# GAT merge of a four-layer graph kernel: two accumulators of three planes, one for VectorE and one for Pool, joined by TensorE in the division

## The chip, the cores and the metric

The kernel runs on one core of one Trainium2 chip. The time is the device time of that core in microseconds, the median of three runs. A profile is one further execution, taken by the hardware profiler, and has its own time.

Engine names: PE is TensorE (PEld are its weight loads), DVE is VectorE, ACT is ScalarE, POOL is GpSimd (Pool), SP issues the transfers.

## The reference, cut to what matters

3125 nodes with 128 features and 103125 edges (`src`, `dst`, sorted by `dst`, self loops included) pass four layers: a graph convolution, an additive attention, a GAT with two heads, and a SchNet-like interaction. The change is in the GAT (and in buffers that the layers share):

```python
xl = (h @ Wl + bl).reshape(n, H, D)          # H = 2, D = 128
xr = (h @ Wr + br).reshape(n, H, D)
e = jax.nn.leaky_relu(xl[src] + xr[dst], NEG_SLOPE)
alpha = jnp.einsum('ehd,hd->eh', e, att)
alpha = _segment_softmax(alpha, dst, n)      # exp(a - max) / (sum + 1e-16) over each dst
msg = xl[src] * alpha[..., None]
out = jax.ops.segment_sum(msg, dst, num_segments=n).mean(axis=1)
out = out + h @ res_W + bias
return residual + out
```

## The kernel before, in words

Nodes are padded to N = 3200 (25 blocks of 128). Edges are cut into 202 tiles of 512. As `dst` is sorted, a tile touches a window of WIN = 20 neighbouring nodes, whose first node is the tile's base (`base_i`). Where all edges lie in their windows one pass does (`k.passes` is 1 at run time); otherwise the stages of a layer run once for each window offset, in a device loop.

**Stages.** A `Stage` is a block with its own semaphores; all engines meet at its end. The GAT layer is: two normalisations, `project` ("sides", which also clears accumulators), `attend` (the attention loop), `merge_gat`, `divide_gat`.

**The attention loop** (`attend`, L1940) goes over the 202 tiles in a software pipeline (`over_tiles`), where each engine works in one step at different tiles. Pool gathers source rows (L888) into a ring of eight buffers; TensorE makes scores, weights and sums; VectorE finds the greatest score of a tile and head. For each tile it leaves three things: `partial`, the weighted sums of the tile's window for each head (128 features on the partitions, 20 columns a head), with weights exp(score - tile's top); `weight_sum`, the sums of the weights; and the tile's tops. Two VectorE instructions keep the tops (`best_of_nodes`): L2220 copies the tile's top in each window cell from PSUM to `rows`, and L2223 takes the running maximum of each node into `node_top`.

**The merge** (`merge_gat`, L2251) brings all tiles to the nodes' common top. Tiles go in groups of GROUP = 24 (`over_groups`): eight full groups and one of ten. The body gets several groups at once, each some rounds behind; the first and last rounds are unrolled, the middle ones are a device loop over pairs of rounds. Columns of a group are its tiles' windows side by side, 24 x 20 = 480. For one group:

- *lower* (L2272): for each tile, 2x20 elements, its row of tops minus `node_top` at its window. VectorE does the first 12 tiles, Pool the other 12.
- ScalarE takes the exponential of the group's row (L2335).
- *columns* (`scale_columns`, L2242): VectorE spreads `weight_sum` over the cells, 128x480.
- *spread*: TensorE spreads each head's factors to 128 partitions with a row of ones (L2348, two matmuls, each profiled as two records) and turns the columns into rows of sums (L2350).
- VectorE multiplies the sums' row by the factors (L2306, 2x480) and `partial` by them, one head at a time (L2310, 128x480, in place).
- *add*: for each tile, VectorE adds 128 x 2 x 20 to `acc` at the window (L2322), and Pool adds 2x20 of the sums' row to `node_sum` (L2363). An engine's adds go one after the other, each waiting for the one before, as neighbouring windows can overlap.

A round lowers the group `now` and adds the group `past`, two groups behind. VectorE and Pool each do 24 adds and 12 lowerings a round, in three batches of eight adds and four lowerings; ahead of a batch the engine reads its 12 window bases from memory into registers (`window_bases`). In a round `now`'s columns are made after these two waits:

```python
dve.wait_ge(spread_ready, past.g + 1)      # TensorE has spread group `past`
wait_count(dve, spread_ready, now.g - 1)   # the columns' buffer (two halves) is free
```

**The division** (`divide_gat`, L2411). TensorE turns the row sums (25 blocks of 2x128, L2425), and then, in seven chunks of up to four blocks, three planes of each: both heads of `acc` and the residual part in `fb` (L2433, 75 transposes). VectorE takes the inverses, adds the residual plane (L2472) and the first head times its inverse (L2476); ScalarE multiplies the second head (L2444), and Pool adds it to `x` (L2455). Chunks alternate between two sets of banks.

Another stage has a role in the prediction: `collect_sums` (L2936), which adds three tables with fp32 matmuls against the identity, `start` on the first and `stop` on the last (L2964, four blocks and three tables a unit). In `project`, VectorE's L635 and Pool's L673 subtract rounded pieces, both with two operands in SBUF.

## Time and profile before

| | |
|---|---|
| median of three runs | 4929.67 us (4923.24 to 4929.72) |
| the profiled execution | 4951.51 us, its span 4949.7 us |
| attention loop of the GAT | 2058.0 to 3406.8 us of the span |
| merge | 3406.8 to 3534.4 us |
| division | 3534.4 to 3553.5 us |
| busy over the span | PE 3993 us (81%), DVE 2863 (58%), ACT 1738 (35%), POOL 2830 (57%) |
| granted TensorE clock | 0.85 mean; 1.0 is 2.4 GHz, 0.5 is 1.2 GHz |

A row of the timeline gives the start, the busy time, the engine, the line and operation, output and inputs, the count, and in brackets the idle time before it and what ended that. A row of a source line gives the least, median and greatest duration in ns. Starts are in us from the start of the span. A row of a stretch gives its bounds and length, then for PE, PEld, DVE, ACT and POOL the busy time and (x) the instructions, and last the granted clock, the DMA share and GB/s. A row of costliest groups gives busy time in us and mean ns, then the idle time ahead and what ended it.

### The profile page before, as it was taken

The page shows a single profiled execution, that of the slowest core. Times are in us where ns is not written, and L with a number is a line of the kernel's source. Part 1 is how long each engine was busy: PE and PEld are TensorE (multiplying, and loading weights), DVE is VectorE, ACT ScalarE, POOL GpSimd, SP SyncE. Part 2 cuts the span into 40 slices and gives each one's busy share as a digit, 9 for nine tenths or more (in the row PEclk, how much of TensorE's full clock was granted, in tenths as well). Part 3 has the DMA queues.
Part 4 walks back from the last instruction along what each step waited for, and adds up shares of the span by engine and source line. Part 5 has one row for each costly group of instructions (what it writes and reads, how often), then busy time and mean ns, then how long its engine had stood idle before and what let it go on. Part 6 is the DMA issues. An engine that isn't in the chain of part 4 may idle for free. (4 is left out here: it accounts for less than half of the span.)

```text
span 4949.7 us, 89651 instructions
## 1 busy us (share of the span) xinstructions
PE 3993.3 (81%) x22463; PEld 2250.2 (45%) x22566; DVE 2862.7 (58%) x8478; ACT 1738.1 (35%) x4474; POOL 2829.9 (57%) x3055
## 2 busy tenths in 40 slices
PE   3996927878878787488888888886479999999987
PEld 1344424444444454244444444442246556556652
DVE  7994032333333334555555555555678888888868
ACT  3773033344344344333333333331222222222226
POOL 0122355666666663555555555554368888888862
PEclk8997967777777777688888888887689999999999
DMA  2322522222222221333333333331056666666660
GB/s 79 97 80 87 160 70 55 57 55 57 55 56 56 56 57 29 110 87 95 96 94 95 95 96 93 95 95 31 1 106 104 105 104 104 104 105 104 105 109 14
DMA packets 377425, 402.41 MB, mean 81 GB/s; under 512 B 86457, under 2 KB 322502, under 8 KB 377030
## 3 DMA queue, kind: packets, MB, share of 16 engines
q0 software_dynamic: 151904, 198.72, 20.8%
q1 hardware_dynamic: 225382, 202.21, 14.3%
q8 instruction: 43, 0.70, 0.1%
q14 instruction: 96, 0.79, 0.1%
HBM read 312.91 MB, written 87.78 MB: 81 GB/s over the span
## 5 line engine op out<-in xcount | busy, mean ns | idle before, releaser
L888 POOL DMA_INDIRECT gathered<-table,sources x952 | 907.0, 953 | 611.8 <-issue 258.9
L1676 POOL DMA_INDIRECT sums<-gathered,idx x606 | 989.9, 1634 | 217.1 <-issue 166.7
L1538 PE MATMUL bank<-wide 128*128 128x512 bf16 x3533 | 829.1, 379 | 5.6 <-issue 0.2
L2195 DVE TENSOR_REDUCE neg_raw<-bank 80x1 f32<-80x512 f32 (+1 forms) x404 | 276.7, 685 | 727.5 <-DMA dst_pair<-local_rows 277.4
L888 POOL DMA_INDIRECT wide<-table,sources x464 | 440.0, 948 | 284.4 <-issue 123.6
L2145 ACT ACTIVATE msg<-bank,neg_top 80x512 f32<-80x512 f32 (+1 forms) x404 | 275.9, 683 | 716.6 <-issue 376.0
L1538 PEld LDWEIGHTS bank<-wide 128*128 128x128 bf16 x3636 | 347.7, 98 | 364.1 <-issue 1.6
L1212 POOL TENSOR_TENSOR acc<-acc,msg 128x20 f32 x404 | 108.7, 269 | 419.6 <-issue 245.7
L2188 DVE TENSOR_TENSOR zact<-zact,bank 128x512 f32<-128x512 f32 x404 | 259.5, 684 | 121.8 <-ACT zact L2137 79.8
L2073 PE MATMUL bank<-zact,att_cells 128*32 128x512 f32 x808 | 287.5, 750 | 46.6 <-issue 45.8
L2055 PEld LDWEIGHTS bank<-ident,gathered 128*128 128x128 f32 x1360 | 196.6, 169 | 272.3 <-issue 248.9
L2076 PE MATMUL bank<-zact,att_cells 128*80 128x512 f32 x404 | 302.7, 841 | 9.2 <-issue 9.2
L2213 DVE COPY edge_rows<-bank 128x320 f32<-128x320 f32 (+1 forms) x404 | 183.3, 454 | 179.1 <-remote 109.2
L2055 PE MATMUL bank<-ident,gathered 128*128 128x128 f32 x1360 | 243.7, 322 | 35.6 <-issue 23.8
L2111 PE MATMUL bank<-edge_rows,gathered 128*128 128x80 f32 x1088 | 185.1, 326 | 102.2 <-DVE edge_rows L2213 91.6
L888 POOL DMA_INDIRECT h_nm<-table,sources x200 | 190.4, 952 | 133.5 <-DMA wide<-table,sources 68.1
L1159 DVE TENSOR_SCALAR gathered<-iota_c,partial 128x500 f16<-128x500 f16 x812 | 265.1, 349 | 2.4 <-issue 1.4
L2086 PE MATMUL bank<-ident,msg 80*128 80x80 f32 (+1 forms) x1616 | 209.3, 256 | 64.8 <-issue 29.0
L2157 ACT COPY partial<-bank 32x20 f32 (+1 forms) x808 | 133.1, 165 | 347.0 <-remote 250.5
L1168 PE MATMUL bank<-gathered,zact 128*128 128x500 f16 x812 | 209.2, 380 | 53.9 <-ACT zact L1275 28.2
L2137 ACT ACTIVATE zact<-bank 128x512 f32<-128x512 f32 x404 | 216.9, 588 | 94.7 <-DMA window<-parts 77.6
L1589 ACT COPY gathered<-bank 128x437 f32<-128x437 f32 x202 | 106.2, 525 | 336.7 <-PE bank L1564 245.3
(394 smaller groups left out, 7612.2 us busy)
## 6 DMA issues: line engine op xcount, KB each, us to landing
zact<-in_src_flat SPq DMA_DIRECT2D x202, 192.0 KB
edge_rows<-in_attr_rows SPq DMA_DIRECT2D x202, 128.0 KB
dst_pair<-local_rows SPq DMA_DIRECT2D x177, 128.0 KB
gathered<-table,sources POOLq DMA_INDIRECT x952
dst_pair<-local_rows SPq DMA_DIRECT2D x202, 64.0 KB
counts<-wide SPq DMA_DIRECT2D x4, 3000.0 KB
counts<-fm_ab SPq DMA_DIRECT2D x4, 3000.0 KB
fm_ab<-counts SPq DMA_DIRECT2D x4, 3000.0 KB
```

The source lines that it names most:

```text
L888: pool.indirect_dma_start(out=g[:, j, :], out_offset=None, in_=table, in_offset=bass.IndirectOffsetOnAxis(ap=mine, axis=0)).then_inc(rows_ ...
L1159: hot = dve.tensor_scalar(k.cell_hot[slot][:, j, :], k.iota_c[:, :], k.cell[:, q], None, ALU.is_equal)
L1538: pe.matmul(k.bank[b][:, :], k.split[t.two][:, c, :], k.source_hot[t.two][:, b * CHUNK:(b + 1) * CHUNK], start=first, stop=c == PARTS - 1, ...
L1676: pool.indirect_dma_start(out=k.sums[j], out_offset=bass.IndirectOffsetOnAxis(ap=k.idx[t.slot][:, j:j + 1], axis=0), in_=out_rows(t)[:, j, ...
L2055: pe.matmul(z_bank(t, h)[:, j * P:(j + 1) * P], g[:, j, h * F:(h + 1) * F], k.ident[:, :], is_transpose=True, start=(j == 0), stop=False, ...
L2073: mm = pe.matmul(score_bank(t)[own_cells(h), :], a.att[h][:, own_cells(h)], k.zact[t.two][:, h, :], start=False, stop=True, skip_group_che ...
L2076: mm = pe.matmul(score_bank(t), a.att[0][:, :], k.zact[t.two][:, 0, :], start=False, stop=True)
L2086: mm = pe.transpose(weight_bank(t)[:, j * cells:(j + 1) * cells], raised(t)[:, j * P:(j + 1) * P], k.ident[lanes(t), lanes(t)])
L2137: act.mul(k.zact[t.two][:, h, :], z_bank(t, h)[:, :], 0.2).then_inc(slope_ready, 1)
L2145: act.activation(raised(t), score_bank(t), ACT.Exp, bias=k.neg_top[lanes(t), bass.ds(t.t, 1)], accum_out=k.weight_sum[lanes(t), bass.ds(t. ...
L2188: m = dve.tensor_tensor(za, za, z_bank(t, h)[:, :], ALU.max)
L2195: dve.tensor_reduce(raw, score_bank(t), AX.X, ALU.max, negate=True).then_inc(top_found, 1)
```

## The change

- There are two accumulators of three planes (head 0, head 1, row sums on partitions 32 and 33): `planes`, the first three planes of one tensor `four` that now holds `acc`, `fa` and `fb`, and `more_planes`, in a new tensor `arena` that also holds `h`, the gathered rows, `dst_pair` and `onehot_t` of the attention loop. VectorE adds the first half of a group's tiles to `planes`, Pool the second half to `more_planes`, each in one instruction of 128 x 3 x 20.
- The scaled parts of a group are written to `scaled` (two halves) and no longer in place.
- The attention loop doesn't copy the tops to `rows`. The merge remakes them from `neg_top`: a second `scale_columns`, one more TensorE matmul and a ScalarE copy into `tops`. A round now has `ahead` (columns, tops), `now` one group behind (lowering, exponential, spread) and `past` three groups behind (multiply, add).
- Lowering adds `node_top` to the negative top, and the exponential has scale -1.
- Bases are read 12 at a time, twice a round.
- After the groups VectorE joins the first accumulator with the arena in a loop of `k.passes` steps of 60 columns and subtracts the arena's part from itself; with one pass this is one step.
- The division reads both accumulators: each transpose of a head or of the row sums becomes two accumulating matmuls against the identity.
- Clears move: Pool clears the arena in five pieces at the end of the attention loop, `node_top` is set at that loop's start on VectorE; `neg_top` is cleared in "sides", and the upper part of `dst_pair` in "xj".

```diff
-    k.h = k.sb("h_nm", [P, B, F])
-    k.fab = k.sb("fm_ab", [P, 2, N])
+    k.arena = k.sb("arena", [P, 3 * N])
+    k.h = k.arena[:, 0:N].rearrange("p (b f) -> p b f", f=F)
+    k.four = k.sb("four", [P, 4, N])
+    k.acc, k.fab = k.four[:, 0:2, :], k.four[:, 2:4, :]
     k.fa, k.fb = k.fab[:, 0, :], k.fab[:, 1, :]
-    k.acc = k.sb("acc", [P, 2, N])
+    k.planes, k.more_planes = k.four[:, 0:3, :], k.arena[:, :].rearrange("p (z n) -> p z n", z=3)
...
+                if gat:
+                    assert k.tiles % ring == 2 and ring == DEEP + 2
+                    n, at = k.n_nodes, k.ring_at
+                    pool.wait_ge(sums_ready, k.tiles - 6)
+                    pool.memset(k.arena[:, at[2]:at[4]], 0.0).then_inc(cleared, 1)
+                    pool.wait_ge(sums_ready, k.tiles - 2)
+                    pool.memset(k.arena[:, 0:n], 0.0).then_inc(cleared, 1)
+                    pool.wait_ge(score_ready, k.tiles)
+                    pool.memset(k.arena[:, at[4]:3 * n], 0.0).then_inc(cleared, 1)
+                    pool.wait_ge(sums_ready, k.tiles - 1)
+                    pool.memset(k.arena[:, at[0]:at[1]], 0.0).then_inc(cleared, 1)
+                    pool.wait_ge(sums_ready, k.tiles)
+                    pool.memset(k.arena[:, at[1]:at[2]], 0.0).then_inc(cleared, 1)
+                    pool.wait_ge(cleared, 5)
...
-                    dve.tensor_copy(k.rows[0:heads, bass.ds(t.t * WIN, WIN)], top_bank(t)).then_inc(top_kept, 1)
-                    wait_count(dve, best, t.t)
+                    dve.wait_ge(best, t.t + 1)
...
+        def lower_and_add(eng, now, past, side, planes):
+
+            for lo in range(0, share, batch):
+                lowers = range(0, 0) if now is None else range(lo, min(lo + batch, now.size // 2))
+                adds = range(0, 0) if past is None else range(lo, min(lo + batch, past.size // 2))
+                tops = window_bases(k, eng, now.t + side * now.size // 2 + lo, len(lowers)) if lowers else []
+                ends = window_bases(k, eng, past.t + side * past.size // 2 + lo, len(adds)) if adds else []
+                for n in range(batch):
+                    if n < len(adds):
+                        i = side * past.size // 2 + adds[n]
+                        wait_count(eng, added[side], past.g * share + adds[n])
+                        w = planes[:, :, bass.ds(ends[n], WIN)]
+                        eng.tensor_tensor(w, w, k.scaled[past.par][:, :, i * WIN:(i + 1) * WIN],
+                                          ALU.add).then_inc(added[side], 1)
+                    if n < len(lowers):
+                        i = side * now.size // 2 + lowers[n]
+                        if lowers[n] == 0:
+                            eng.wait_ge(tops_kept, now.g + 1)
+                            wait_count(eng, scaled, now.g - 1)
+                        m = eng.tensor_tensor(k.lowered[now.par][:, i * WIN:(i + 1) * WIN],
+                                              k.tops[now.par][:, i * WIN:(i + 1) * WIN],
+                                              k.node_top[:, bass.ds(tops[n], WIN)], ALU.add)
+                        if lowers[n] == now.size // 2 - 1:
+                            m.then_inc(lowered[side], 1)
...
+                def spread_and_add(ahead, now, past):
                     if past is not None:
                         n = past.size * WIN
+                        out = k.scaled[past.par]
                         dve.wait_ge(spread_ready, past.g + 1)
+                        wait_count(dve, added[0], (past.g - 1) * share)
+                        wait_count(dve, added[1], (past.g - 1) * share)
+                        dve.tensor_tensor(out[k.sum_lanes, 2, 0:n], k.lowered[past.par][:, 0:n],
+                                          k.bank[4 + past.par][0:heads, 0:n], ALU.mult)
                         for h in range(heads):
+                            m = dve.tensor_tensor(out[:, h, 0:n],
+                                                  a.partial[:, h, bass.ds(past.t, past.size), :].rearrange(
+                                                      "p t n -> p (t n)"),
+                                                  k.bank[h * 2 + past.par][:, 0:n], ALU.mult)
                         m.then_inc(scaled, 1)
+                    if ahead is not None:
+                        wait_count(dve, tops_ready, ahead.g - 1)
+                        wait_count(dve, spread_ready, ahead.g - 1)
+                        scale_columns(k, dve, a, top_columns(ahead), k.neg_top, ahead)
+                        scale_columns(k, dve, a, sum_columns(ahead), k.weight_sum, ahead).then_inc(columns_ready, 1)
                     if past is not None:
                         dve.wait_ge(scaled, past.g + 1)
+                    lower_and_add(dve, now, past, 0, k.planes)
+                over_groups(dve, k.tiles, (0, 1, 3), spread_and_add)
+                dve.wait_ge(added[0], total)
+                dve.wait_ge(added[1], total)
+                size = 3 * k.n_nodes // ceil_div(k.n_nodes, WIN)
+                mine = k.planes.rearrange("p z n -> p (z n)")
+                with dve.Fori(0, k.passes) as n:
+                    cols = bass.ds(n * size, size)
+                    dve.tensor_tensor(mine[:, cols], mine[:, cols], k.arena[:, cols], ALU.add).then_inc(joined, 1)
+                    dve.wait_ge(joined, n + 1)
+                    dve.tensor_tensor(k.arena[:, cols], k.arena[:, cols], k.arena[:, cols], ALU.subtract)
 
             @block.scalar
             def _(act):
+                def keep_and_raise(ahead, now):
+                    if ahead is not None:
+                        n = ahead.size * WIN
+                        act.wait_ge(tops_ready, ahead.g + 1)
+                        for eng_lowered in lowered:
+                            wait_count(act, eng_lowered, ahead.g - 1)
+                        act.copy(k.tops[ahead.par][:, 0:n], k.bank[6 + ahead.par][0:heads, 0:n]).then_inc(tops_kept, 1)
+                    if now is not None:
+                        m = k.lowered[now.par][:, 0:now.size * WIN]
+                        act.wait_ge(lowered[0], now.g + 1)
+                        act.wait_ge(lowered[1], now.g + 1)
+                        act.activation(m, m, ACT.Exp, scale=-1.0).then_inc(raised, 1)
+                over_groups(act, k.tiles, (0, 1), keep_and_raise)
 
             @block.tensor
             def _(pe):
+                def spreads(ahead, now):
+                    if ahead is not None:
+                        n = ahead.size * WIN
+                        pe.wait_ge(columns_ready, ahead.g + 1)
+                        wait_count(pe, tops_kept, ahead.g - 1)
+                        pe.matmul(k.bank[6 + ahead.par][0:heads, 0:n], a.own[:, :],
+                                  top_columns(ahead)[0:a.lanes, 0:n], start=True, stop=True).then_inc(tops_ready, 1)
+                    if now is not None:
+                        n = now.size * WIN
+                        pe.wait_ge(raised, now.g + 1)
+                        wait_count(pe, scaled, now.g - 1)
+                        for h in range(heads):
+                            pe.matmul(k.bank[h * 2 + now.par][:, 0:n], k.head_row[:, h * P:(h + 1) * P],
+                                      k.lowered[now.par][:, 0:n], start=True, stop=True)
+                        pe.matmul(k.bank[4 + now.par][0:heads, 0:n], a.own[:, :], sum_columns(now)[0:a.lanes, 0:n],
+                                  start=True, stop=True).then_inc(spread_ready, 1)
+                over_groups(pe, k.tiles, (0, 1), spreads)
...
                 for b in range(B):
-                    mm = pe.transpose(k.bank[7][:, b * heads:(b + 1) * heads], k.node_sum[:, b * P:(b + 1) * P],
-                                      k.ident[k.sum_lanes, k.sum_lanes])
+                    out, cols = k.bank[7][:, b * heads:(b + 1) * heads], slice(b * P, (b + 1) * P)
+                    pe.matmul(out, k.node_sum[:, cols], k.ident[k.sum_lanes, k.sum_lanes], start=True, stop=False)
+                    mm = pe.matmul(out, k.more_planes[k.sum_lanes, 2, cols], k.ident[k.sum_lanes, k.sum_lanes],
+                                   start=False, stop=True)
                 mm.then_inc(sums_turned, 1)
                 for i, (lo, hi) in enumerate(cs):
                     wait_count(pe, divided, i - 1)
                     wait_count(pe, headed, i - 1)
-                    for n, src in enumerate(srcs):
+                    for n in range(heads):
                         for b in range(lo // P, hi // P):
-                            mm = pe.transpose(k.bank[n * 2 + i % 2][:, b * P - lo:(b + 1) * P - lo],
-                                              src[:, b * P:(b + 1) * P], k.ident[:, :])
+                            out, cols = k.bank[n * 2 + i % 2][:, b * P - lo:(b + 1) * P - lo], slice(b * P, (b + 1) * P)
+                            pe.matmul(out, k.acc[:, n, cols], k.ident[:, :], start=True, stop=False)
+                            pe.matmul(out, k.more_planes[:, n, cols], k.ident[:, :], start=False, stop=True)
+                    for b in range(lo // P, hi // P):
+                        mm = pe.transpose(k.bank[heads * 2 + i % 2][:, b * P - lo:(b + 1) * P - lo],
+                                          k.fb[:, b * P:(b + 1) * P], k.ident[:, :])
                     mm.then_inc(ready, 1)
```

In the middle part the removed lines of the four engines' programs are left out; they are in the code above.

## Rows read from the trace of the kernel before

**Rows 1.** Busy time of each engine in three stretches: attention loop, merge, division.

```profile
2058.00:3406.80 1348.80, 1107.76 (x7683) 578.07 (x7683) 736.41 (x2025) 416.08 (x1018) 768.32 (x808) 0.86 0.33 93
...
3406.80:3534.40 127.60, 44.37 (x54) 11.21 (x54) 76.18 (x344) 5.18 (x9) 66.79 (x298) 0.50 0.00 1
...
3534.40:3553.50 19.10, 13.50 (x100) 12.21 (x100) 11.88 (x35) 7.13 (x25) 8.05 (x7) 0.83 0.00 1
```

**Rows 2.** Timeline of the merge, one group of tiles.

```profile
3458.34 0.64 DVE L2306 TENSOR_TENSOR zact<-wide,bank 2x480 f32<-2x480 f32 x1
...
3459.01 1.22 DVE L2310 TENSOR_TENSOR partial<-partial,bank 128x480 f32 x2
...
3459.52 0.60 ACT L2335 ACTIVATE wide<-wide  x1 [13.51 <-POOL wide L2272]
...
3460.15 0.65 DVE L2242 TENSOR_TENSOR msg<-weight_sum,place 128x480 f32<-128x480 f32 x1
...
3460.36 0.49 PEld L2348 LDWEIGHTS bank<-wide,head_row 2*128 2x128 f32 x2 [10.62 <-issue]
...
3460.36 3.56 PE L2348 MATMUL bank<-wide,head_row 2*128 x4 [8.95 <-DVE partial L2310]
...
3461.32 0.33 PEld L2348 LDWEIGHTS bank<-wide,head_row 2*128 2x128 f32 x1 [0.47 <-issue]
...
3463.85 1.76 PE L2350 MATMUL bank<-msg,own 128*2 128x480 f32 x2
```

**Rows 3.** Timeline of the merge, VectorE's adds, unrolled and in the loop.

```profile
3437.19 0.20 DVE L2322 TENSOR_TENSOR acc<-acc,partial 128x40 f32 x1 [0.94 <-DVE acc L2322]
...
3437.52 0.53 DVE L2322 TENSOR_TENSOR acc<-acc,partial 128x40 f32 x2
...
3466.61 0.20 DVE L2322 TENSOR_TENSOR acc<-acc,partial  x1 [0.17 <-DVE acc L2322]
...
3467.02 0.20 DVE L2322 TENSOR_TENSOR acc<-acc,partial  x1
```

**Rows 4.** Timeline of the merge, Pool's adds (a lowering between).

```profile
3470.05 0.21 POOL L2363 TENSOR_TENSOR fm_ab<-fm_ab,zact 2x20 f32 x1 [0.85 <-POOL fm_ab L2363]
...
3470.61 0.22 POOL L2363 TENSOR_TENSOR fm_ab<-fm_ab,zact 2x20 f32 x1
```

**Rows 5.** One source line: Pool's adds in the division.

```profile
L2455 POOL TENSOR_TENSOR x_nm<-x_nm,wide x7: 454/1272/1279, 3542.8 to 3552.8; 128x512 f32<-128x512 f32 x6, 128x128 f32<-128x128 f32 x1
```

**Rows 6.** Timeline of the division, TensorE.

```profile
3535.10 2.82 PE L2425 MATMUL bank<-ident,fm_ab 2*128 2x2 f32 x25 [17.54 <-PEq L909]
...
3544.54 1.06 PE L2433 MATMUL bank<-ident,acc 128*128 128x128 f32 x8 [0.26 <-DVE x_nm L2476]
```

**Rows 7.** Timeline of the stage that collects the sums, TensorE.

```profile
4818.45 1.95 PE L2964 MATMUL bank<-ident,wide 128*128 128x128 f32 x16
...
4821.13 1.95 PE L2964 MATMUL bank<-ident,wide 128*128 128x128 f32 x16
```

**Rows 8.** Busy time in two stretches: TensorE's clock in division and collection.

```profile
3538.00:3542.00 4.00, 4.00 (x24) 3.84 (x24) 2.00 (x6) 1.15 (x4) 0.00 (x0) 0.66 0.01 4
...
4814.00:4818.00 4.00, 3.82 (x20) 3.82 (x21) 0.00 (x0) 0.00 (x0) 0.00 (x0) 0.58 0.94 313
```

**Rows 9.** Timeline of the projection "sides", Pool and VectorE.

```profile
2045.97 1.16 POOL L673 TENSOR_TENSOR gathered<-gathered,h_nm 128x512 f32<-128x512 f32 x1 [1.01 <-ACT h_nm L653]
...
2046.45 1.23 DVE L635 TENSOR_TENSOR gathered<-gathered,h_nm 128x512 f32<-128x512 f32 x1 [0.28 <-ACT h_nm L656]
```

**Rows 10.** Costliest groups of the attention loop, two of VectorE's.

```profile
L2195 DVE TENSOR_REDUCE neg_raw<-bank 64x1 f32<-64x512 f32 x202 | 138.8, 687 | 313.1 <-DMA dst_pair<-local_rows 277.4 <-PE bank L2073 34.0
...
L2220 DVE COPY wide<-bank 2x20 f32 (+1 forms) x202 | 35.0, 173 | 15.7 <-DMA wide<-table,sources 1.7 <-issue 1.3 <-PE bank L2095 0.4
```

**Rows 11.** A source line of Pool's memsets, and the timeline of the loop's end.

```profile
L669 POOL MEMSET acc<- x2: 5433/5435/5437, 657.2 to 2016.3; 128x6400 f32 x2
...
3400.53 1.07 PE L2107 MATMUL bank<-h_nm,edge_rows 128*32 128x128 f32 x16
```

140 lines of the change are left out of this document (44 added, 96 removed).

## The prediction

> **What bounds the kernel now.** I began with the busy time by stretch [rows 1]. The profiled execution took 4951.51 us, 1.8 us more than its span. Three stretches touch the change. The GAT attention loop (1349 us) is untouched but for one VectorE instruction a tile and its last microseconds. The merge (127.6 us) is the stage that is rewritten. The division (19.1 us) gets more matmuls. In the merge TensorE runs at its lower clock (0.50) and is busy 44 us, VectorE 76, Pool 67: no engine is full, so what counts is who waits for whom.
>
> The timeline of one group of 24 tiles shows that [rows 2]. ScalarE idles 13.5 us and works 0.60, so a group takes 14.1 us. TensorE starts when the exponential is there and runs 3.56 + 1.76 us, 5.25 from first start to last end. Its result is wanted only in the next round, so this 5.25 lies beside VectorE's and Pool's own work. VectorE multiplies (0.64 + 1.22), makes one set of columns (0.65), then has 24 adds and 12 lowerings, as Pool has. An add, a lowering and an add start 0.33 us after each other where the code is unrolled and 0.41 in the loop [rows 3]; each new set of bases costs a gap of 0.94. Pool needs 0.56 for the same pair and a gap of 0.85 [rows 4]. Both engines are near their own limit.
>
> **The change part by part.**
>
> *Merge, the adds.* VectorE and Pool now have 12 adds and 12 lowerings each, in two batches. A VectorE add grows from 40 to 60 columns: 0.02 us more by the multiply of 480 in about 0.61 [rows 2], so a pair is 0.35 unrolled and 0.43 looped; 12 pairs and two gaps of 0.9 are 6.0 and 7.0 us. A Pool add goes from 2x20 (0.22) to 128x60. Pool's 128x512 and 128x128 adds take 1.27 and 0.45 [rows 5], 2.1 ns a column, so 60 columns are about 0.31 and a pair 0.67: with its start (1.3) and one gap a round is 10.2 us.
>
> *Merge, a new wait.* The row-sum columns are now made in the round of `ahead`, while the same group is lowered one round later (`now`). The buffer has two halves, so making columns for group g waits until TensorE has spread g-2, and g-2 was lowered at the end of the round just before. The old code made and lowered in one round and had a whole round of slack there. Behind this wait stand VectorE's columns, all its adds and its lowerings, and for these lowerings the next exponential waits. The loop is therefore serial: signal 0.2, exponential 0.60, signal 0.2, TensorE 5.25 [rows 2], 6.3 in all; the three multiplies (1.9) and Pool's share hide in it. Then two sets of columns, 1.3, then 6.0 or 7.0 of adds. A round is 13.6 unrolled and 14.6 in the loop, against 10.2 for Pool, which so has slack.
>
> The stage: columns, tops through TensorE and ScalarE and the first lowerings, about 7.1; chain 6.3, columns 1.3 and the next lowerings 2.9: 17.6 before the first adds. Six held rounds, three at 13.6, two at 14.6, one with a short last group at 13.0: 83.0. The last three rounds have no columns, and Pool, whose adds follow each other at 0.50 when nothing lies between, is last: 11 + 8 + 3.5 = 22.5. Joining the accumulators, one pass of a loop, is 2.5 by estimate from two 60-column operations (0.25 each) and its reads. Sum 125.6, against 127.1 from the stage's first to its last instruction.
>
> *Contention.* Pool's adds now have full width beside two-operand adds of VectorE. A VectorE operation of 128x512 with two SBUF operands took 1.23 us with a Pool operation beside it for 0.68 of that [rows 9]; by the multiply above it would be about 0.67 alone. So nearly the whole overlap was lost. Pool moves data some 0.13 us per add; a quarter to a half of these meet an add. I take 0.5 us a round, +3 (bounds 0 and +10, where Pool too becomes slower and the round is Pool's). The Trainium skill (GPSIMD Engine Reference, Specifications) says that Pool shares its SBUF interfaces with VectorE and contends with instructions that have two SBUF inputs; the trace agrees in this one row pair. The merge comes to +1.5.
>
> *Division.* 75 transposes and 25 small ones become 25 transposes and 150 matmuls, since a sum of two planes needs accumulating fp32 matmuls. The same form stands in the stage that collects the sums: twelve of them (four blocks, three tables) every 2.68 us at the full clock, 0.223 each [rows 7]; each is two records (16 for eight), where a transpose is one. Transposes are 0.133 each [rows 6]. A chunk of four blocks goes from 12 transposes (1.6, hidden under VectorE's 1.8) to 16 x 0.223 + 4 x 0.133 = 4.1. TensorE becomes the bound: 6 x 4.1 + 1.0 = 25.6. The row sums: 25 in 2.82 become 50 matmuls. At the low clock two weight loads of full form from two partitions span 0.49 and one takes 0.33 [rows 2], so they stand 0.17 apart and a matmul takes 0.34; at the full clock I take 0.22. The clock rose about 5.5 us after the stage's start [rows 6, 8]. 16 cold and 34 warm are 13.0. With 1.4 behind the last matmul: 40.0, against 18.2: +21.8. Lower bound: two loads at the transposes' pace (0.113), halved once warm, 8.3 for the row sums, +17. Upper: the clock rises only when wide matmuls come; in the other stage it stood at 0.58 over the first 4 us [rows 8]; 17.0 and 1.5 for a cold first chunk, +27.
>
> By the Trainium skill (TensorE: Matmul & The Clock Gate, LDWEIGHTS) a weight load goes by its columns, not its rows, 0.107 us for 128. The 25 small transposes agree (0.113 each). By that rule the row sums at two loads each would cost 10.7 and the division be 2.3 us shorter.
>
> *Attention loop.* The copy of the tops to `rows` goes (202 x 0.17) [rows 10]. VectorE idles there 313 us ahead of its first reduction, waiting for others; TensorE is busy 1108 of 1349 us. I take -2; bounds 0 and -38. The added memset of `node_top` (2x3200, about 2.7) lies in VectorE's wait for the first loads; its old place on Pool lay beside an equal one on VectorE: 0.
>
> *Clears on Pool at the loop's end.* Five memsets at 0.85 ns a column [rows 11]. The 3200 columns wait for the sums that end at 3401.6, then 2304, 1024 and 1024: 2.7 + 2.0 + 0.9 + 0.9 and signals is 3408.5, against 3406.6 now: +2 (bounds 0, +3). `neg_top` and `dst_pair` clears ahead of projections: +0.3, since Pool's first subtraction comes later anyway.
>
> Sum: -2 + 2 + 0.3 + 1.5 + 21.8 = +23.6. The profiled execution would be 4975. It lay 22 us above the median of the runs, so I move the median: 4929.7 + 23.6 = 4953.
>
> **The rivals.**
> - *The merge isn't held.* If the columns find TensorE done, a round is Pool's 10.2 to 10.8, six rounds save 19 to 20 us: +3, 4933, no change. For it: this is the overlap the two engines' counts would allow. Against: the wait's count and TensorE's 5.25.
> - *The division is cheap.* If the matmuls cost as transposes do, TensorE needs 5.5 for the row sums and 2.5 a chunk, +3 in place of +21.8: 4935, no change. Rows 7 speak against it.
> - *The copy sat on the attention loop's path.* Then each tile gains the copy and its start, 0.19: -38, in all -13, 4917, faster. It decides from 0.16 us a tile on. For it: the copy stands ahead of the weights that TensorE's sums need. Against: VectorE's 313 us of idle [rows 10].
> - *Pool and VectorE slow each other* beyond what I took: rounds of 15.2 set by Pool, +10: 4963, slower. By the skill's rule this is what two-input adds on both engines would do; the row pair shows the size only for wide operations.
>
> **How the numbers follow.** A measurement of this kernel can tell 0.2%, 10 us, from no change. Chances: forecast 0.66, contention 0.12, merge not held 0.07, division cheap 0.07, copy on the path 0.08. So slower 0.78, same 0.14, faster 0.08. The range goes from the two cases of no change, 4932, to 4968, the upper bound of the division with part of the contention; only the faster case and the sums of several extremes are left out. For the forecast alone it is 4944 to 4964.
>
> **What would show it.** In the profile after: `columns` (the second set) on VectorE idles about 4 us until the last matmul of the round, in six rounds; ScalarE's exponentials stay 13 to 15 us apart; Pool idles some 3 us a round on `scaled`; VectorE's adds take 0.22, Pool's 0.31. The division's stretch is near 40 us with TensorE full and VectorE waiting for it. The attention loop's length is unchanged within 3 us. Wrong it would be if the division's matmuls overlap better than in the stage I took them from, if the loop's length moves (202 tiles make 10 us of 0.05), or if Pool's full-width adds are far from 0.31.

## The result and the profile after

The changed kernel took 4968.09 us (median of 4, 4967.64 to 4969.75) against 4927.51 for the kernel before (now a median of 4 as well): the difference of the medians is 40.6 us. The ratio on record is 1.0088, 95% interval 1.0075 to 1.0100, that is 37 to 49 us slower. The direction was right, the size was not: +23.6 had been forecast, and the median lies 0.1 us above the range's upper end of 4968.

The profiled execution of after took 4969.75 us, 1.7 off its median; that of before had lain 22 us above its own. So the two profiles are compared stage by stage, not by their spans. Busy time by stretch of the kernel after (columns as in [rows 1]); attention loop, a stretch in between that was not there before, merge, division:

```profile
2045.80:3379.10 1333.30, 1107.33 (x7683) 578.58 (x7683) 710.85 (x1822) 414.21 (x1018) 772.58 (x812) 0.87 0.33 94
3379.10:3387.20 8.10, 0.00 (x0) 0.00 (x0) 0.00 (x0) 0.00 (x0) 1.62 (x2) 0.66 0.00 1
3387.20:3520.70 133.50, 59.08 (x72) 12.01 (x72) 62.37 (x249) 9.89 (x18) 52.92 (x202) 0.51 0.00 1
3520.70:3573.00 52.30, 48.32 (x325) 48.07 (x325) 13.06 (x39) 7.93 (x26) 8.02 (x7) 0.76 0.00 1
```

Read against [rows 1]. On one basis (first operation of a stage to the first of the next): VectorE's idle in front of the merge 0.32 before, 8.20 after; merge 128.2 (3406.91 to 3535.10) and 133.5; division 18.6 (3535.10 to 3553.73) and 51.5 (3520.76 to 3572.24). That is +7.9, +5.3 and +32.8, +46.0 in all, inside the interval of the medians. The attention loop is judged further down; from its first to its last copy of the sums it took 1286.9 us in the profile of before and 1271.6 in this one.

**In front of the merge.** Timeline of the loop's end: Pool's memsets and VectorE's operations on either side of the gap.

```profile
3374.20 2.77 POOL L2060 MEMSET arena<- 128x3200 f32 x1 [14.97 <-PE bank L2133]
...
3376.91 2.02 POOL L2062 MEMSET arena<- 128x2304 f32 x1
...
3378.87 0.96 POOL L2064 MEMSET arena<- 128x1024 f32 x1
3378.89 0.20 DVE L2254 COPY partial<-bank 128x40 f32<-128x40 f32 x1 [1.49 <-PE bank L2145]
3379.76 0.96 POOL L2066 MEMSET arena<- 128x1024 f32 x1
3387.29 0.66 DVE L2269 TENSOR_TENSOR edge_rows<-neg_top,place 128x480 f32<-128x480 f32 x1 [8.20 <-PEq L2035]
```

The bracket is VectorE's idle time ahead of the merge. The memsets take what was forecast and end 1.6 us behind VectorE. The other 6.6 us stand in a view that shows the engines' sequencers as well: the source line that opens the stage's block. Its columns are count, shortest, median and longest in ns, first and last start.

```profile
L2035 DVEq DRAIN  x1: 236/236/236, 3378.9 to 3378.9; - x1
L2035 POOLq COMPARE_BRANCH  x1: 33/33/33, 3380.8 to 3380.8; - x1
L2035 POOLq DRAIN  x1: 5881/5881/5881, 3381.1 to 3381.1; - x1
L2035 SPq EVENT_SEMAPHORE  x1: 17/17/17, 3387.2 to 3387.2; - x1
```

The same line of the kernel before:

```profile
L2022 POOLq DRAIN  x1: 9565/9565/9565, 3378.2 to 3378.2; - x1
L2022 ACTq DRAIN  x1: 289/289/289, 3405.7 to 3405.7; - x1
```

A drain is what an engine's sequencer records at the end of a stage. Here Pool's took 5.9 us after the change and 9.6 before, where the other engines' took 0.24 to 0.29. In both profiles only three of Pool's drains took more than 0.2 us, each at the end of a stage in which Pool gathers or scatters rows by index; what it waits for in them is not shown. Before, the drain ended 19 us ahead of the others' last. Now the clears stand in front of it, and everybody waits.

**The merge.** Timeline of the first held round after: VectorE's held columns, Pool beside them, the first adds.

```profile
3410.51 0.66 DVE L2269 TENSOR_TENSOR edge_rows<-neg_top,place 128x480 f32<-128x480 f32 x1 [4.15 <-PE bank L2391]
3410.53 0.79 POOL L2309 TENSOR_TENSOR arena<-arena,wide 128x60 f32 x1
3411.09 0.75 DVE L2269 TENSOR_TENSOR msg<-weight_sum,place 128x480 f32<-128x480 f32 x1
...
3412.39 0.22 DVE L2309 TENSOR_TENSOR four<-four,wide 128x60 f32 x1 [0.55 <-issue]
3412.60 0.17 DVE L2316 TENSOR_TENSOR wide<-wide 2x20 f32<-2x20 f32 x1
3412.75 0.22 DVE L2309 TENSOR_TENSOR four<-four,wide 128x60 f32 x1
```

The first add of each of the two batches in the last held round, then the exponentials in front of and behind the six held rounds:

```profile
3488.64 0.22 DVE L2309 TENSOR_TENSOR four<-four,zact 128x60 f32 x1 [1.10 <-issue]
...
3493.74 0.22 DVE L2309 TENSOR_TENSOR four<-four,zact 128x60 f32 x1 [2.68 <-issue]
```

```profile
3404.49 0.60 ACT L2372 ACTIVATE zact<-zact 2x480 f32<-2x480 f32 x1 [0.47 <-DVE zact L2316]
...
3495.88 0.60 ACT L2372 ACTIVATE zact<-zact 2x480 f32<-2x480 f32 x1 [7.10 <-DVE zact L2316]
```

The forecast wait is there: columns held 4.0 to 4.2 us in six rounds (and 6.3 in the first), a VectorE add takes 0.22 and Pool's 0.31, where [rows 3, 4] have 0.20 and 0.22. What is new is the 2.68 us between a round's two batches of adds, where the kernel before had 0.94 to 1.2. The exponentials at 3404.49 and 3495.88 have six rounds between them: 91.4, where 83.0 was forecast. Each round took 15.0 to 15.4 us, in the loop and outside it. Pool is slowed where VectorE makes columns: its add beside them took 0.79 us, not 0.31 (3410.53); Pool has slack there.

**The division.** TensorE's timeline: row sums (each of the fifty matmuls is two records), then wide matmuls cold and warm.

```profile
3530.17 0.56 PE L2460 MATMUL bank<-ident,four 2*128 2x2 f32 x2
3530.59 0.56 PE L2461 MATMUL bank<-ident,arena 2*128 2x2 f32 x2
3531.02 0.56 PE L2460 MATMUL bank<-ident,four 2*128 2x2 f32 x2
...
3542.18 0.80 PE L2470 MATMUL bank<-ident,four 128*128 128x128 f32 x2
...
3546.54 0.39 PE L2470 MATMUL bank<-ident,four 128*128 128x128 f32 x2
...
3546.76 0.39 PE L2471 MATMUL bank<-ident,arena 128*128 128x128 f32 x2
```

Row-sum matmuls start 0.427 apart (3530.17, 3530.59, 3531.02), so fifty take 21.3 us. Wide ones start 0.427 apart too at the lower clock, and 0.22 apart at the full one, as in [rows 7]; a chunk then takes 4.01. The clock by stretch (the number ahead of the last two of a line):

```profile
3536.00:3540.00 4.00, 4.00 (x21) 4.00 (x20) 0.00 (x0) 0.00 (x0) 0.00 (x0) 0.50 0.00 0
3542.00:3545.00 3.00, 3.00 (x15) 2.98 (x15) 0.87 (x3) 0.00 (x0) 0.00 (x0) 0.50 0.00 0
3545.00:3548.00 3.00, 3.00 (x27) 3.00 (x27) 0.00 (x0) 0.00 (x0) 0.00 (x0) 0.91 0.02 5
```

TensorE was busy without a gap for 21 us of row sums at 1.2 GHz, and went to 2.4 about 3 us after the wide matmuls began.

### The profile page after: what moved, and what is told of

Same layout as the page of the kernel before. It is cut to its first block and busy times, and to the rows that moved or that the text cites. A ratio compares the mean times of both kernels' runs of the same rounds, so it can differ in the third digit from the quotient of the medians.

```text
span 4968.0 us, 89212 instructions
## 1 busy us (share of the span) xinstructions
PE 4039.8 (81%) x22809; PEld 2286.2 (46%) x22809; DVE 2824.7 (57%) x8182; ACT 1743.0 (35%) x4483; POOL 2820.9 (57%) x2967
## 5 line engine op out<-in xcount | busy, mean ns | idle before, releaser
L901 POOL DMA_INDIRECT arena<-table,sources x1152 | 1094.6, 950 | 734.4 <-issue 310.5
L1689 POOL DMA_INDIRECT sums<-arena,idx x606 | 989.0, 1632 | 217.3 <-issue 168.9
L2082 PEld LDWEIGHTS bank<-ident,arena 128*128 128x128 f32 x1760 | 242.1, 164 | 314.3 <-issue 292.7
L1225 POOL TENSOR_TENSOR four<-four,msg 128x20 f32 x404 | 108.7, 269 | 420.8 <-issue 246.2
L2082 PE MATMUL bank<-ident,arena 128*128 128x128 f32 x1760 | 300.8, 315 | 33.9 <-issue 16.9
L1172 DVE TENSOR_SCALAR arena<-iota_c,partial 128x500 f16<-128x500 f16 x812 | 258.1, 337 | 2.7 <-issue 1.7
L2137 PE MATMUL bank<-edge_rows,arena 128*128 128x80 f32 x1088 | 182.3, 322 | 89.0 <-DVE edge_rows L2241 70.2
L1181 PE MATMUL bank<-arena,zact 128*128 128x500 f16 x812 | 209.6, 381 | 53.9 <-ACT zact L1288 28.1
L1457 DVE TENSOR_SCALAR arena<-arena,iota_w,always 128x512 bf16<-128x512 bf16 x556 | 233.0, 419 | 17.2 <-DMA arena<-local_rows 13.7
L1602 ACT COPY arena<-bank 128x437 f32<-128x437 f32 x202 | 106.1, 525 | 336.7 <-PE bank L1577 249.6
```

Of the source, the lines that this page charges most:

```text
L901: pool.indirect_dma_start(out=g[:, j, :], out_offset=None, in_=table, in_offset=bass.IndirectOffsetOnAxis(ap=mine, axis=0)).then_inc(rows_ ...
L1172: hot = dve.tensor_scalar(k.cell_hot[slot][:, j, :], k.iota_c[:, :], k.cell[:, q], None, ALU.is_equal)
L1457: return dve.tensor_scalar(hot, row, k.iota_w[:, 0:1], k.always[:, 0:1], ALU.is_equal, ALU.max)
L1689: pool.indirect_dma_start(out=k.sums[j], out_offset=bass.IndirectOffsetOnAxis(ap=k.idx[t.slot][:, j:j + 1], axis=0), in_=out_rows(t)[:, j, ...
L2082: pe.matmul(z_bank(t, h)[:, j * P:(j + 1) * P], g[:, j, h * F:(h + 1) * F], k.ident[:, :], is_transpose=True, start=(j == 0), stop=False, ...
```

## The experiments

They ran in three sets. In the first two the kernel before took 4400 to 4401 us, at a mean granted clock of 0.91, in the third 4956, at 0.85, so a run is compared with the kernel before of its own set alone. The attention loop, from its first to its last copy of the sums, took 992 to 995 us in the first two, at a granted clock of 0.99 to 1.00, and 1284 to 1286 in the third, at 0.87 to 0.88; merge and division don't differ so. The first and the third set carry the same chip number, so the chip alone does not explain the two levels, and their cause stays open. "Over before" is the difference of the medians; "idle" is VectorE's idle in front of the merge; "merge and division" runs from the merge's first operation to the start of the last batch statistic behind the division (151.5 in the first profile of before, 189.6 in that of after).

| run | over before, us | ratio, 95% interval | idle | merge and division |
|---|---|---|---|---|
| before_again | profile only | | 0.3 | 151.8 |
| after_again | +41.8 | 1.0096 (1.0079 to 1.0113) | 8.2 | 189.6 |
| e1_unheld | +25.3 | 1.0058 (1.0041 to 1.0075) | 8.2 | 168.0 |
| e2_sums_by_dve | +33.2 | 1.0081 (1.0065 to 1.0098) | 8.2 | 175.1 |
| e3_two_clears | +41.2 | 1.0098 (1.0081 to 1.0115) | 4.1 | 190.0 |
| e4_batches_of_4 | +27.2 | 1.0063 (1.0047 to 1.0080) | 8.2 | 172.7 |
| e5_sums_third | +47.3 | 1.0110 (1.0093 to 1.0126) | 8.2 | 191.4 |
| e6_after_with_copy | +44.8 | 1.0104 (1.0087 to 1.0121) | 8.2 | 189.6 |
| e7_clears_in_merge | +33.1 | 1.0066 (1.0046 to 1.0085) | 0.3 | 190.8 |
| e8_loads_of_8 | +49.2 | 1.0094 (1.0073 to 1.0116) | 8.2 | 193.2 |
| e9_pool_joins_a_head | +18.2 | 1.0044 (1.0029 to 1.0059) | 8.1 | 167.6 |
| e10_all | -24.8 | 0.9952 (0.9936 to 0.9968) | 0.3 | 126.3 |

**The two kernels again.** No edit.

> The kernel before, unchanged, for a second profile. The first profiled execution of it took 4951.5 us against a median of 4929.7. If those 22 us lie in the attention loop, this one shows a loop some 20 to 26 us shorter than 1349 (1323 to 1329) and the same merge (128) and division (19) within 0.3 us; then the change's cost can be read stage by stage. If they lie in the merge or the division, those two stages are shorter here, and the change cost more in them than the two profiles show.

> The changed kernel, unchanged, beside the kernel before on the chip of this set, as the base for the other runs of the set. From the stages read so far: 8.2 us of gap in front of the merge against 0.3, the merge 133.5 against 128.2, the division up to the last batch statistic 56.1 against 23.3, the attention loop unchanged; so 44 to 48 us slower than the kernel before.

Merge and division of before came out as in its first profile (128.1 and 18.9). The loop, between its first and its last copy of the sums, took 993.0 us here, and 991.9 in the changed kernel. The second profile stands at the shorter level and so does not say where the 22 us of the first lay; the difference of 18.2 us between the two first spans is the stages' +46.0 less some 28 us ahead of the merge, which the medians do not confirm.

**The copy in the attention loop.**

```diff
                     dve.wait_ge(top_turned, t.t + 1)
+                    dve.tensor_copy(k.tops[0][:, t.slot * WIN:(t.slot + 1) * WIN], top_bank(t))
                     dve.wait_ge(best, t.t + 1)
```

> The changed kernel with the copy of the tops (2 x 20, one a tile, on VectorE) put back into the attention loop, into a place that nothing reads. Theory 1, the copy was never on the loop's path: the loop stays within 3 us of that of the changed kernel. Rival, it sat on the path: 202 copies at 0.17 to 0.19 us make the loop 34 to 38 us longer. In between, a part of it is on the path (VectorE is less idle on a chip where the loop takes 995 us than where it takes 1287).

The loop took 994.4 us; in the six changed kernels of these two sets without the copy it took 991.9 to 995.0. The copy costs nothing there. At the longer level it was not tried. Without the copy the loop took 1271.6 us in the first profile of after and 1284 to 1286 in four runs of the third set, with it 1286.9 in the first profile of before: 1 to 15 us less, not the 38 of the rival.

**The held wait.**

```diff
                     if ahead is not None:
                         wait_count(dve, tops_ready, ahead.g - 1)
-                        wait_count(dve, spread_ready, ahead.g - 1)
-                        scale_columns(k, dve, a, top_columns(ahead), k.neg_top, ahead)
-                        scale_columns(k, dve, a, sum_columns(ahead), k.weight_sum, ahead).then_inc(columns_ready, 1)
+                        scale_columns(k, dve, a, top_columns(ahead), k.neg_top, ahead).then_inc(columns_ready, 1)
+                    if now is not None:
+                        wait_count(dve, spread_ready, now.g - 1)
+                        scale_columns(k, dve, a, sum_columns(now), k.weight_sum, now).then_inc(sums_ready, 1)
...
+                        pe.wait_ge(sums_ready, now.g + 1)
```

> The changed kernel with one edit: the row-sum columns of a group are made one round later, in the round in which the group is lowered, so that their buffer is free when VectorE comes to it; the same instructions otherwise. Theory 1, the merge is held by that wait (six rounds with an idle of 4.0 to 4.2 us in front of the columns): the idle goes, a round falls from 15.2 to 11.0 us, and the kernel becomes 20 to 26 us faster than the changed one, 4942 to 4948 us. Rival, VectorE and Pool set the round by their own work and slow each other: the freed time comes back as idle on the multiplies or as longer adds, rounds stay at 14 us or more and less than 8 us are won.

The merge fell from 133.5 to 111.0 us; the kernel's distance from before fell by 16.5 (each with some 7 us of uncertainty, and its loop was 3 us longer than that of after_again). The wait was the bound. A round is now 12.1 us (the mean of the last five), not 11.0: with both engines adding at the same time each pair of VectorE goes at Pool's pace. Timeline of e1, both engines in a batch:

```profile
2905.53 0.29 POOL L2310 TENSOR_TENSOR arena<-arena,wide 128x60 f32 x1
2905.57 0.34 DVE L2310 TENSOR_TENSOR four<-four,wide 128x60 f32 x1
...
2906.01 0.31 POOL L2310 TENSOR_TENSOR arena<-arena,wide 128x60 f32 x1
2906.04 0.36 DVE L2310 TENSOR_TENSOR four<-four,wide 128x60 f32 x1
```

A pair takes 0.49 and an add 0.35, against 0.36 and 0.22 alone. This is the contention that the prediction had priced; in the changed kernel the median of VectorE's adds is 0.22 us, since the wait keeps the two engines' adds apart for the most part. The rule quoted there from the Trainium skill (GPSIMD Engine Reference, Specifications) is borne out by these rows, at the size of an add of 60 columns.

**The gap between batches.**

```diff
-    batch = share // 2
+    batch = share // 3
```

> The changed kernel with one number changed: a round's 12 adds and 12 lowerings stand in three batches of 4, not two of 6, so the window bases are loaded three times, 4 + 4 of them, not twice, 6 + 6. VectorE's gap between two batches was 2.7 us; in the kernel before, with 8 + 4 bases, it was 0.9 to 1.2. Theory 1, each such gap is a fixed wait for the loads: a third batch adds 2.7 us a round and the held rounds go from 15.2 to 17.9, 16 us slower. Theory 2, the gap grows with the bases (12 of them 2.7): two gaps of 1.8, 3.6 in all, the round 0.9 longer, 5 us slower. Theory 3, loads of 4 and 8 are cheap and loads of 6 dear: two gaps of 0.9, the round 0.9 shorter and the gap behind the columns shorter too, 5 to 10 us faster.

A third batch made the merge 16.8 us shorter (116.7). The gaps between the batches of VectorE are 0.58 and 0.73. Then loads of eight where six are used, for the adds' bases too:

```diff
-                tops = window_bases(k, eng, now.t + side * now.size // 2 + lo, len(lowers)) if lowers else []
...
+                more = {batch: 8}
+                tops = window_bases(k, eng, now.t + side * now.size // 2 + lo,
+                                    more.get(len(lowers), len(lowers))) if lowers else []
...
```

> The changed kernel with one edit: where six window bases are loaded for a batch, eight are loaded and six used, at the same addresses; batches of 6 as in the changed kernel. Batches of 4 were 15 to 17 us faster. Theory 1, a load of six is dear and a load of four or eight is cheap: the gap between the batches falls from 2.7 to about 1 us, a held round from 15.2 to 13.5, 10 us are won. Theory 2, the place matters (the loads begin at multiples of 6, not of 4 or 8): the gap stays at 2.7 or more. Theory 3, the number of bases in flight: the gap grows to 3.6.

The merge became 3.7 us longer. Timeline of a round of e8, behind the columns and between the batches:

```profile
3460.24 0.22 DVE L2312 TENSOR_TENSOR four<-four,zact 128x60 f32 x1 [0.20 <-issue]
...
3466.09 0.22 DVE L2312 TENSOR_TENSOR four<-four,zact 128x60 f32 x1 [3.75 <-issue]
```

The loads have records of their own, under the source line of the helper that issues them (columns as above). In turn: one round of the changed kernel (two batches, so four loads), and the whole merge of e4, of e8 and of the kernel before:

```profile
L1188 DVEq TENSOR_LOAD <-base_i x4: 817/1118/1418, 3441.1 to 3446.3; - x4
```

```profile
L1188 DVEq TENSOR_LOAD <-base_i x52: 314/344/368, 2861.7 to 2974.8; - x52
```

```profile
L1188 DVEq TENSOR_LOAD <-base_i x34: 593/620/1859, 3419.2 to 3550.7; - x34
```

```profile
L1175 DVEq TENSOR_LOAD <-base_i x53: 342/534/604, 3406.9 to 3532.8; - x53
```

Four bases from a multiple of four cost 0.34 us, eight from such a place 0.60. Six cost 0.82 from a multiple of four (VectorE's first batch of group g begins at tile 24g) and 1.42 from elsewhere (its second, at 24g + 6). Eight from there cost 1.86. In the short last group VectorE's five bases begin at 192 and cost 0.61, Pool's five at 197 and cost 1.17, in the same place of the program. So a load that begins off a multiple of four costs 0.23 a base, although 24g + 6 to 24g + 11 hold a whole aligned four; one that begins on it costs 0.34 for four and 0.23 for each base left over (0.80 for six, nearly). A round's four loads are 4.5 us in the changed kernel and 4.9 in e8, its six loads in e4 are 2.1: 2.4 us less in each of six held rounds are 14 of the 16.8. Two loads of 1.4 are the gap of 2.7, two of 1.86 that of 3.75, two of 0.34 that of 0.6 to 0.7. So number and place both count: the third theory of e4 had the sign and half the size or less, and in e8 the second and the third were each half of it.

**The end of the attention loop.** First, the last three clears left out; then the clears moved into the merge.

```diff
                     pool.memset(k.arena[:, 0:n], 0.0).then_inc(cleared, 1)
-                    pool.wait_ge(score_ready, k.tiles)
-                    pool.memset(k.arena[:, at[4]:3 * n], 0.0).then_inc(cleared, 1)
...
-                    pool.wait_ge(cleared, 5)
+                    pool.wait_ge(cleared, 2)
```

> The changed kernel with one edit: of Pool's five clears at the end of the attention loop only the first two are left (3200 columns and a ring slot pair); the other three regions of the second accumulator keep what was in them, so this leaves out a part of the zeroing. Pool's last memset now ends about 2 us before VectorE's last copy of the loop, not 1.6 after it. Theory 1, the next stage waits for something that Pool does after its last instruction and that takes about 6.6 us (3380.7 to 3387.3 in the profile after): the gap in front of the merge shrinks only by what Pool is earlier, from 8.2 to about 4.5 us, and 3.7 us are won. Rival, the next stage waits only for the clears themselves, which end later than the profile draws them: the gap falls to the 0.3 us of the kernel before and 8 us are won.

```diff
+                pool.memset(k.arena[:, 0:n], 0.0).then_inc(cleared, 1)
                 def second_half(now, past):
+                    if past is not None and isinstance(past.g, int) and past.g == 0:
+                        pool.memset(k.arena[:, at[0]:at[2]], 0.0).then_inc(cleared, 1)
+                        pool.memset(k.arena[:, at[4]:3 * n], 0.0).then_inc(cleared, 1)
+                        pool.wait_ge(cleared, 3)
```

> The changed kernel with one edit: of Pool's five clears only the early one (two ring slots, six tiles before the end) stays in the attention loop; the others stand in the merge, 3200 columns at its start and the rest before Pool's first add, where Pool idles (3.8 us at the start, some 7 us before the first add). Theory 1, the next stage waits for what Pool does behind its last instruction of a stage, about 6.6 us: with Pool idle long before the loop's end, the gap in front of the merge is 0.3 us again, the merge keeps its 133.4 us, and 8 us are won against the changed kernel (4442.5 in the last set, 41.8 over the kernel before), so 34 us over the kernel before. Rival, the gap is the stage's own (more semaphores, a longer stage entry): it stays at 5 us or more and less than 3 us are won.

The first operation of the merge in e3 and in e7 (the bracket is the idle in front):

```profile
2857.34 0.66 DVE L2263 TENSOR_TENSOR edge_rows<-neg_top,place 128x480 f32<-128x480 f32 x1 [4.12 <-PEq L2035]
```

```profile
3409.16 0.66 DVE L2261 TENSOR_TENSOR edge_rows<-neg_top,place 128x480 f32<-128x480 f32 x1 [0.33 <-PEq L2035]
```

Pool's drain took 5.77 us in both; in e3 it began at 2851.3, 1.9 ahead of the end of VectorE's last copy, and so cost 4.1; in e7 it began 17.8 us ahead, at 3390.8, and cost nothing. By the stages e3 won 3.7 us and e7 6.7, by their distances from before 0.6 and 8.7, each with some 7 us of uncertainty; here the stages decide.

**The division.** Three runs: row sums joined by VectorE; the fifty matmuls of the row sums behind two chunks; row sums joined by VectorE and one head by Pool, which TensorE then turns with four transposes a chunk.

```diff
+                dve.tensor_tensor(k.node_sum, k.node_sum, k.more_planes[k.sum_lanes, 2, :],
+                                  ALU.add).then_inc(plane_joined, 1)
...
+                pe.wait_ge(plane_joined, 1)
                 for b in range(B):
-                    pe.matmul(out, k.node_sum[:, cols], k.ident[k.sum_lanes, k.sum_lanes], start=True, stop=False)
-                    mm = pe.matmul(out, k.more_planes[k.sum_lanes, 2, cols], k.ident[k.sum_lanes, k.sum_lanes],
-                                   start=False, stop=True)
+                    mm = pe.transpose(k.bank[7][:, b * heads:(b + 1) * heads], k.node_sum[:, b * P:(b + 1) * P],
+                                      k.ident[k.sum_lanes, k.sum_lanes])
```

> The changed kernel with one edit: VectorE adds the second accumulator's row-sum plane onto the first (2 partitions x 3200) at the start of the division, and TensorE turns the sum with 25 small transposes in place of 50 matmuls. Theory 1, the row sums' matmuls cost 0.43 us each at the lower clock and stand alone on the path (21.3 us in the profile after): VectorE's add takes about 4.2 (3200 columns at 1.3 ns, from 0.67 for 512), the transposes 2.8, so 14 us are won, 4954 us. The clock then rises in the middle of the first chunk as it does now. Rival, the cost of the division sits in the chunks (TensorE-bound at 3.95 each against 1.78): then less than 5 us are won here.

Merge and division fell by 14.5 us. The add and the 25 transposes:

```profile
2991.88 3.48 DVE L2502 TENSOR_TENSOR four<-four,arena 2x3200 f32<-2x3200 f32 x1 [0.99 <-PEq L922]
2995.41 2.73 PEld L2461 LDWEIGHTS bank<-ident,four 2*128 2x128 f32 x25 [19.24 <-DVE four L2502]
2995.41 2.82 PE L2461 MATMUL bank<-ident,four 2*128 2x2 f32 x25 [18.51 <-DVE four L2502]
```

```diff
                 for i, (lo, hi) in enumerate(cs):
+                    if i == 2:
+                        for b in range(B):
+                            ...
```

> The changed kernel with one edit: TensorE makes the first two chunks of the division (wide matmuls and transposes) ahead of the 50 small matmuls of the row sums, not behind them; the same work. Theory 1, the row sums cost 0.43 us each because the clock stays at its lower level while TensorE does nothing else: behind 4 to 8 us of wide matmuls they meet the full clock, cost 0.21 each, and 10 us are won, less what the first chunks cost cold. Rival, small matmuls do not hold the clock either: it falls again in their course, and less than 4 us are won; the row sums stay near 20 us. The granted clock in the stretch of the row sums tells the two apart.

The clock of e5, in two stretches of wide matmuls, three from the row sums' start at 3002.2 on, and one of the third chunk:

```profile
2996.00:2998.00 2.00, 2.00 (x15) 2.00 (x15) 0.00 (x0) 0.00 (x0) 0.00 (x0) 0.75 0.00 0
2998.00:3000.00 2.00, 2.00 (x20) 2.00 (x19) 0.00 (x0) 0.00 (x0) 0.00 (x0) 1.00 0.00 0
...
3002.00:3005.00 3.00, 3.00 (x28) 2.83 (x26) 0.00 (x0) 0.00 (x0) 0.00 (x0) 1.00 0.00 0
3005.00:3010.00 5.00, 5.00 (x35) 5.00 (x34) 0.00 (x0) 0.00 (x0) 0.00 (x0) 0.72 0.00 0
3010.00:3015.00 5.00, 5.00 (x26) 5.00 (x25) 0.00 (x0) 0.00 (x0) 0.00 (x0) 0.50 0.02 3
...
3023.00:3025.00 2.00, 2.00 (x11) 2.00 (x11) 0.79 (x4) 0.00 (x0) 1.52 (x2) 0.50 0.00 0
```

The rival held: the small matmuls did not hold the clock, it fell in their course, and the third chunk met the lower clock again. The fifty took 16.8 us, not 21.3, but TensorE then waited 3.0 us for VectorE, and merge and division became 1.8 us longer. A small matmul took 0.223 us at the full clock and 0.427 at the lower, as much as a wide one. By the Trainium skill (TensorE: Matmul & The Clock Gate, LDWEIGHTS) a load goes by its columns and not its rows; that small and wide cost the same agrees, at either clock.

```diff
+                def join(i):
+                    if i < len(cs):
+                        h = k.acc[:, 1, cs[i][0]:cs[i][1]]
+                        pool.tensor_tensor(h, h, k.more_planes[:, 1, cs[i][0]:cs[i][1]],
+                                           ALU.add).then_inc(head_joined, 1)
+                join(0)
+                join(1)
                 for i, (lo, hi) in enumerate(cs):
+                    join(i + 2)
...
```

> The changed kernel with the division of the run in which VectorE joins the row sums, and further: Pool adds the second accumulator's plane of the second head onto the first, a chunk at a time and two chunks ahead, so that TensorE turns that head with four transposes, not eight matmuls. Theory 1, the chunks are TensorE's at 3.95 us: a chunk now takes 8 matmuls at 0.223 and 8 transposes at 0.133, 2.85, so six chunks win 6.6 us, and with the row sums' 14.5 it is 21 us faster than the changed kernel: the division up to the last batch statistic takes 35 us, and the kernel is 20 to 21 us over the kernel before. Rival, Pool becomes the bound (a join and an addition of 1.28 each, and VectorE's adds beside it slow both): a chunk takes 3.3 us or more, and less than 4 us are won beyond the row sums.

22 us were won in the two stages, 7.5 beyond e2. A chunk takes 2.66 us: 1.78 for eight matmuls, 0.88 for eight transposes that follow each other at 0.11.

**All together.**

The edits of e1, e4, e7 and e9 in one kernel.

> All that helped, in one kernel: the columns of the row sums a round later, batches of 4, the clears in the merge, and the division with the row sums joined by VectorE and the second head by Pool. If the gains add up where they lie in different stages, the gap in front of the merge is 0.3, the division 35 us against 23.4, and the merge is bound by the two engines' own adds: VectorE's and Pool's pairs of add and lowering follow each other at 0.49 us when both work, 12 of them 5.9, with the multiplies 1.9, the columns 1.3 and gaps of 0.7 a round is about 10.5 us and the merge some 98 us against 128.2. That is 18 us faster than the kernel before, 4383 against 4401. Rival, without the held wait the engines slow each other more or the exponential and TensorE's 5.3 us come back into the round: the merge stays at 108 us or more and the kernel is within 8 us of the kernel before.

The merge took 96.6 us with the joining add of the sums in it (busy time by stretch, merge and division):

```profile
3408.10:3504.70 96.60, 55.44 (x72) 12.57 (x72) 72.44 (x250) 9.79 (x18) 61.44 (x207) 0.56 0.00 1
3504.70:3534.60 29.90, 21.45 (x175) 21.20 (x175) 17.21 (x61) 8.40 (x26) 14.56 (x13) 0.79 0.01 1
```

The kernel is 25 us faster than the one before (16 to 32 by the interval; 18 had been expected), and some 67 faster than the changed one, each counted from the kernel before of its set. The gains added up: without the join of the sums (4.6 us and 1.0 ahead of it) the merge is 91, 42 shorter than the changed kernel's, where e1 and e4 alone had won 22 and 17.

## Why the prediction went wrong

- *Held merge: right in its mechanism.* Stage start to the first exponential of the held rounds 17.2 us (forecast 17.6), the last rounds and the join 24.9 (25.0), the wait 4.0 to 4.2 in six rounds (forecast 4). **The term that was mis-sized** is "two gaps of 0.9": the gap behind the columns was 0.5 to 1.1, the gap between batches 2.7, since its two loads of six bases begin off a multiple of four. Six rounds took 91.4, not 83.0; the looped rounds, put at 14.6, and the last, put at 13.0, were as long as the others. The +3 for contention was not needed in the changed kernel. So +5.3 in place of +1.5.
- *Division: the matmul form was right, the row sums' price and clock were not.* Chunks 4.01 us against 4.1. Of "16 cold and 34 warm" all 50 were cold, and each cost 0.427, not 0.34: the price at the lower clock is nearly twice that at the full one (0.223), and the estimate from the weight loads of [rows 2] missed it. The 10.7 us that the prediction gives beside it, two loads a matmul, are half of what was measured. "The clock rose about 5.5 us after the stage's start" was carried from a stage in which wide transposes stood there. 21.3 for 13.0 is 8.3 of the 11.0 by which the division missed; the chunks took 26.9 for 25.6, since the first met the lower clock, and 1.8 lie behind the last matmul (3.2 us, 3.4 before the change, put at 1.4); the division before was 0.4 longer on this basis than the 18.2 taken. The upper bound of +27 had all 50 cold, but at 0.34.
- *Clears at the loop's end: the step that was missing.* "+2" priced the memsets, which came out at 1.6, and not what Pool does behind its last instruction. That drain stood in the trace of before, at 9.6 us, hidden since it ended 19 us ahead of the stage's end. +7.9 in place of +2.
- *Attention loop:* -2 forecast; at the shorter level six changed kernels lie 1 us below to 2 us above before's 993.0, inside their scatter. Projections' +0.3 is not separable.
- *Rivals:* the merge was held, the division was not cheap, the copy was not on the path (tested at the shorter level of the loop), contention did not decide. The contention rival had named rounds of 15.2 us, and the held rounds took 15.2, but by the wait and the loads, not by Pool; that is chance. None of them alone was what moved the time out to 4968; the sum of three mis-sized terms was, 3.8 + 11.0 + 5.9 = 20.7 us, with 1.7 us for the attention loop and the projections 22.4: the stages' 46.0 against the forecast 23.6. The medians' 40.6 lies 5 us under that sum, within their interval; whether the loop itself was a few us shorter in those runs stays open.

## What to carry to other kernels

Work that is moved to an engine's end is priced with what the engine does behind it: look at the sequencers' records of the stage's end, not only at the busy spans. A price is carried to another place only with its state, TensorE's clock and who keeps it up, an address's place, a neighbour's idleness. When a buffer is filled a round earlier, count the rounds of slack that its last reader has left: here moving one operation back by a round was worth 22 us of a merge of 133.

## What was unexpected in the hardware

- Loads of bases into registers cost by where they begin: 0.34 us for four, 0.82 for six and 0.60 for eight from a multiple of four, 1.17 for five, 1.42 for six and 1.86 for eight from elsewhere.
- Pool's drain at the end of the GAT attention stage took 5.8 to 5.9 us in the changed kernels, also where it began 17.8 us ahead of the others' end, and 9.6 and 19.8 in the two profiles of the kernel before; VectorE's, ScalarE's and TensorE's took 0.24 to 0.29.
- Matmuls with two rows and two columns did not raise TensorE's clock in 21 us without a gap, and did not hold it once it was up.
- Adds of 60 columns on VectorE went from 0.22 to 0.35 us beside Pool's of the same size, and the pair of add and lowering fell into Pool's step of 0.49. Pool's add went from 0.31 to 0.79 beside VectorE's columns of 128x480.
